# Eight-piece loading of the second half's projection weights over the value steps, and feed-forward weights issued ahead of the values, in a decoder layer

## The reference

```
x = layernorm(x + relative_position_attention(x))     # 16 heads of 32, over the axis of length 8
x = layernorm(x + cross_attention(context, x, mask))  # 8 heads of 64, 512 keys per batch
x = layernorm(x + feed_forward(x))                    # 512 -> 2048 -> 512, relu, fp8-like rounding
```

## Time and profile before

| | |
|---|---|
| median of 3 runs | 1884.73 us (1884.24 to 1888.88) |
| the profiled execution | 1884.78 us |
| its span, first to last instruction | 1883.0 us |
| mean granted TensorE clock | 0.986 of full |
| TensorE busy | 1786.8 us, 95% |
| VectorE busy | 1369.8 us, 73% |
| ScalarE busy | 771.7 us, 41% |
| GpSimd busy | 562.3 us, 30% |
| phase A ends, phase B begins | at about 819 us of the span |

### The profile page before, as it was taken

The page is one execution under the profiler, slowest core; times in us unless marked ns, Lnnn a source line. Parts: engine busy times, 40 slices in busy tenths (PEclk is TensorE's granted clock), DMA queues, the critical chain, the costliest instruction groups (busy, mean ns, idle before and its releaser), DMA issues. The chain is left out here.

```text
span 1883.0 us, 33021 instructions
## 1 busy us (share of the span) xinstructions
PE 1786.8 (95%) x12476; PEld 984.3 (52%) x12476; DVE 1369.8 (73%) x1454; ACT 771.7 (41%) x1208; POOL 562.3 (30%) x576
## 2 busy tenths in 40 slices
PE   6999999999999998977899999999999999999988
PEld 3665455545654564544545545455454554545543
DVE  2899999999899999857556577575775666757621
ACT  3333222322222222237547266373562754736522
POOL 3135865696449525600100302002011020030010
PEclk9999999999999999999999999999999999999999
DMA  9535456525653467666420613606207153061010
GB/s 214 129 76 137 96 135 151 124 76 143 146 118 84 118 167 156 148 148 194 104 71 2 136 51 52 135 1 121 66 9 139 40 85 102 1 130 34 12 34 23
DMA packets 322653, 183.97 MB, mean 98 GB/s; under 512 B 225583, under 2 KB 278831, under 8 KB 322510
## 3 DMA queue, kind: packets, MB, share of 16 engines
q1 hardware_dynamic: 316448, 178.37, 40.7%
q10 hardware_dynamic: 6062, 3.49, 0.9%
HBM read 94.75 MB, written 33.55 MB: 68 GB/s over the span
## 5 line engine op out<-in xcount | busy, mean ns | idle before, releaser
L1178 POOL TENSOR_TENSOR q<-q,x_hi 128x512 f16<-128x512 f32 x28 | 40.5, 1476 | 599.2 <-ACT x_hi L1525 599.2
L1206 PE MATMUL b_ff<-x2T_hi,w1T_hi 128*128 128x512 f16 x512 | 194.6, 380 | 2.3 <-DVE x2T_lo L1616 2.3
L1206 PE MATMUL b_ff<-x2T_hi,w1T_lo 128*128 128x512 f16 x512 | 194.5, 380 | 0.0
L1206 PE MATMUL b_ff<-x2T_lo,w1T_hi 128*128 128x512 f16 x512 | 194.5, 380 | 0.0
L1616 DVE TENSOR_TENSOR p_lo<-k,p_hi 128x1024 f16<-128x1024 f32 x128 | 161.4, 1261 | 37.1 <-ACT p_hi L1471 37.1
L1504 ACT ACTIVATE k<-b_st,mbias 128x512 f32<-128x512 f32 x256 | 161.9, 693 | 40.8 <-PE b_st L1273 37.9
L1666 DVE SCALAR_TENSOR_TENSOR top<-b_st,mleast,top 128x512 f16<-128x512 f32 x168 | 126.1, 751 | 51.4 <-PE b_st L1233 34.4
L785 DVE TENSOR_TENSOR prod<-q,k 128x4096 f32<-128x4096 f32 x32 | 142.2, 4443 | 21.9 <-ACT q L661 21.1
L578 PE MATMUL sm_b<-cT_hi,wsT_hi 128*128 128x256 f16 x512 | 141.7, 277 | 15.1 <-DMA cT_lo<-rows_lo 13.7
L544 PE MATMUL pj_b<-winT_hi,xT_hi 128*128 128x512 f16 x384 | 147.4, 384 | 1.2 <-DVE winT_lo L852 1.2
L544 PE MATMUL pj_b<-winT_lo,xT_hi 128*128 128x512 f16 x384 | 147.2, 383 | 0.0
(11 more groups left out here) (279 smaller groups left out, 4348.2 us busy)
## 6 DMA issues: line engine op xcount, KB each, us to landing
cn<-in_ctx_dram SPq DMA_DIRECT2D x64, 256.0 KB, 3.1
k<-kT_scratch SPq DMA_DIRECT2D x24, 512.0 KB, 7.9
x<-in_x_dram SPq DMA_DIRECT2D x32, 256.0 KB, 3.1
x_scratch<-x SPq DMA_DIRECT2D x32, 256.0 KB, 2.1
q<-x_scratch SPq DMA_DIRECT2D x8, 1024.0 KB, 5.6
q<-x_scratch SPq DMA_DIRECT2D x32, 256.0 KB, 3.0
out_dram<-q SPq DMA_DIRECT2D x32, 256.0 KB, 3.9
xn<-in_x_dram SPq DMA_DIRECT2D x24, 256.0 KB, 2.9
```

What stands on the lines that cost most here:

```text
L1206: mm = pe.matmul(out, a, c, start=(start and n == 0), stop=end)
```

## The change

The load of `tgt_w` (1 MB, one DMA) and of `xout_w` (2 MB, one DMA) at the end of step 56 become eight pieces, one at the end of each of the steps 56 to 63: first four pieces of `tgt_w` of 128 rows (256 KB each), then four of `xout_w` of 128 rows (512 KB each). The piece of step 61 stands ahead of the x1 load of that step. The wait for `sc_done` stays ahead of the first piece. TensorE's waits for the two loads ask for 64 in place of 16. In phase B the issues of the feed-forward weight pairs 0 and 1 (four DMAs of 256 KB) move from behind `load_heads(0, True)` into it, between the keys and the values.

```diff
-                if g == 16 * (NB - 1) + 8 and w.b_ld is not None:
-                    sp.wait_ge(s["sc_done"], 8 * NB)
-                    sp.dma_start(w.wt_n, d.tgt_w.rearrange("(o p) k -> p o k", p=P)).then_inc(w.b_ld["wt"], 16)
-                    sp.dma_start(w.wx_n, d.xout_w.rearrange("(o p) k -> p o k", p=P)).then_inc(w.b_ld["wx"], 16)
+                o = g - 16 * (NB - 1) - 8
+                if 0 <= o < 8 and w.b_ld is not None:
+                    if o == 0:
+                        sp.wait_ge(s["sc_done"], 8 * NB)
+                    rows_of = slice(o % 4 * P, (o % 4 + 1) * P)
+                    if o < 4:
+                        sp.dma_start(w.wt_n[:, o, :], d.tgt_w[rows_of, :]).then_inc(w.b_ld["wt"], 16)
+                    else:
+                        sp.dma_start(w.wx_n[:, o - 4, :], d.xout_w[rows_of, :]).then_inc(w.b_ld["wx"], 16)
...
                 sp.dma_start(k2[0:D2, :, :], k_in[b, 0]).then_inc(s["k_ld"], 16)
                 if first:
+                    for n in range(2):
+                        load_weights(n)
                     sp.wait_ge(s["made"], 1)
...
             load_heads(0, True)
-            for n in range(2):
-                load_weights(n)
...
                 if n in (0, 4):
-                    pe.wait_ge(w.b_ld["wx" if n else "wt"], 16)
+                    pe.wait_ge(w.b_ld["wx" if n else "wt"], 64)
```

## The result

The changed kernel takes 1892.19 us, the median of eight runs (1887.65 to 1896.06); the kernel before, run beside it on the same chip, 1884.52 us (1880.8 to 1888.88). The ratio is 1.0032, 95% interval 1.0018 to 1.0046. The loss is real and small, some 6 us. It is three times what was forecast, and the time lies above the range.

What follows compares the result with a forecast made beforehand. TensorE, busy for 95% of the span, was taken to bound the kernel, so only its idle gaps count. 0.6 (step 57) + 1.4 (step 61), all else 0, gave +2.0 us: 1884.78 to 1886.8, range 1881.3 to 1890.4.

Steps and rivals of the forecast that it cites:

- the 6.39 us hold: SP held by a transpose issued at 699.35 behind the 2 MB wx_n load; hidden, so its removal is worth 0.
- rival A: The gap before 721.26 came from the big loads after all: 1881.8 us, or 1875.9 with the first gap; chance 0.20.
- steps 58 to 60, 62 and 63: Pieces at these steps delay nothing TensorE waits for (3 us of cover for row 59): cost 0.
- the moved weights are worth 0: Second half, weights 0 and 1 ahead of the values: 2.7 us of queue, covered; 0, bounds -1 and +1 us.
- I take 0.6: Step 57, 256 KB piece ahead of row 55's transposes: 0.6 us, between 0.4 (issue alone) and 1.1 (issue and queue).
- I take 1.4: Step 61, 512 KB piece just ahead of the x1 load: 1.4 us of queue, bounds 0.45 and 3.9.
- the rate row: DMA rate of 385 GB/s in the window 700:705, used to size step 61's 0.52 MB at 1.36 us.
- I add 0: Step 61, more slow clock behind the longer gap: 0 in the sum, 1.3 us kept for the range.
- Rival B: A piece blocks transposes behind it for its whole landing, 3.1 us at step 57, 3.9 at 61: 1891.8; chance 0.10.
- Rival C: Nothing on the path: step 57's piece fits queue holes, step 61's x1 load flows as before: 1884.8 us; chance 0.10.
- the early rows_hi: Sign of being right: ScalarE's rows_hi of row 55 comes some 4 us earlier.
- the unmoved restart: Sign of being right: TensorE's restart at 711.15, behind VectorE's stage_lo, stays where it was.

Runs made afterwards that it cites:

- the second one of the same kernel: The changed kernel, unaltered, timed and profiled once more beside a fresh set of the kernel before: 1889.71 us, ratio 1.0035 (1.0023 to 1.0047).

## Why the prediction was wrong

**Right by its steps.** That the big loads of 697 and the 6.39 us hold were hidden, by VectorE's product and GpSimd's long operation: TensorE's restart moved by 0.14 us, and rival A is dead. That steps 58 to 60, 62 and 63 cost next to nothing: the kernel without the piece of 61 stands at 1.0007, of which step 57 is 1.0 us. That the moved weights are worth 0: 0.9995. That the damage is done at step 61, by a piece ahead of the x1 load that row 63's transposes stand behind, and at step 57: shown by putting in the one piece alone, and by taking the x1 load away, with which the changed kernel stands at 0.9998 and the kernel before at 0.9984.

**Wrong by its sizes.** Three terms were too small, and all of one sign.

- "I take 0.6" at step 57: 1.0, near the upper bound of 1.1. The issue and the queue both counted, 0.5 us each, against the reason that the DMA share of 0.62 left holes.
- "I take 1.4" at step 61: the five profiles with a 512 KB piece have a mean of 11.05 us from the residual to quarter 60, against 8.66 in the five with nothing ahead. That is 2.4, inside the bounds 0.45 and 3.9. Two steps failed here. "SP's own 0.45 us run while the queue is full" left the issue out, but the x1 load was issued 0.47 us later in each of the five and quarter 60 keeps its distance to that load's landing; the four small DMAs delay it by their issuing alone. And the rate row gave 1.36 us for the queue where the landing took 1.9 longer. That row is from 700:705; the earlier trace rows has 268 GB/s in 780:785, and by that rate 0.52 MB would be 2.0 us. It is no better as a rule: 1 MB would be 3.9 where 2.2 were found, and 8 KB brought 1.0 and 1.6.
- "I add 0" for more slow clock: from quarter 60 to the second half it takes 37.24 us at the mean of those five, against 35.96 in the five with nothing ahead. (It takes 35.04 or 35.05 in each of the six profiles that show the full clock from 780 to 800.) That is 1.3, the very figure that was kept for the range and left out of the sum. That the dip was there already was no reason for it to stay as long as it was: before, the granted clock is 0.74, 0.92 and 1.00 in the three windows of 5 us from 780 on; with the 512 KB piece alone 0.72, 0.60 and 1.00; after the change 0.71, 0.50 and 0.77.

These are the terms that were mis-sized. They make 1.0 + 2.4 + 1.3 = 4.7 us where 2.0 was forecast, against 6.0 by the first ratio and 6.6 by the second. The rest, 1.3 to 1.9 us, is inside both intervals, and its cause stays open; the start of the second half was at a lower clock after the change (0.74 against 0.84 in 820:840), but the stretch from its first transposes to the first maximum_row matmul lies between 31.3 and 34.2 us in all these kernels without order, so no cause is named for it. The upper end of the range, 1890.4, had both upper bounds but hardly any clock and nothing for this. With the three middles as found, the sum would have been 1889.5: inside the range, and still under the 0.3% from which on the prediction speaks of slower. So the chance of 0.12 for that was too small, since the sum belonged close to the limit, but the right sizes alone would not have put the forecast beyond it.

**The rivals.** Rival B gave 1891.8, nearest to the measured time, and not for its reason. It wanted 3.1 us at step 57, where the seven profiles have 1.0. At step 61 it wanted 3.9; one profile has that (+3.90), the four others with a 512 KB piece lie 1.5 to 2.3 over the mean of 8.66. The Trainium skill, "SBUF — State Buffer", section "The DMA setup-cost knee", gives each transfer about 2 us whatever its size. For a small transfer by itself the trace agrees: the 8 KB pieces landed 2.5 and 2.6 us after their issue, the four of 8 KB in 2.0 at the median. As a price that is paid anew by each transfer in the queue, which was the rival's reading and is not the page's, it is too high at step 57 and wrong for the four small ones, behind which the x1 load landed in 5.7 us. Rival C fell too.

**The wrong signs that weren't.** The prediction named as a refutation any gap that grows by more than 3 us. The gap ahead of quarter 60 did, by 3.89 us, in the first profile, and by 1.36 in the second one of the same kernel. One profile would have spoken for rival B. Of the signs for being right, the early rows_hi (by 3.9 us), the unmoved restart and the waits of the second half came; the gap before quarter 52 was to be 3.5 to 4 us and was 2.49, for the reason given above.

## What to carry to other kernels

A load that is late nowhere gains nothing by being cut up and spread, and each piece is a new chance to stand ahead of something that is late somewhere: look for the transfers that the idle engine waits for, and put nothing ahead of them; here even 8 KB put TensorE's restart off by 1.5 and 2.1 us, of which 0.47 was the issue. Where a gap has a large load just ahead of its transfer, move that load behind the transfer; here this took some 3 us off the kernel before and 6.4 off the changed one, though the change kept a cost of its own. When a gap is going to grow, price the slow clock behind it by the difference between an execution with the dip and one without, and don't take its presence as a reason for zero.

## What the runs showed of the hardware that was not expected

- TensorE's restart behind row 63 follows the landing of the 1 MB load that stands ahead of the transposes, by 1.8 to 2.0 us in fourteen profiles, whatever stands ahead of that load.
- A DMA of 8 KB ahead of the 1 MB load delayed that restart by 1.5 and 2.1 us, one of 512 KB by 1.5 to 2.3 us in four profiles of five and 4.0 in the fifth. Four of 8 KB delayed it by 1.5 us, all of it SP's issuing; the 1 MB load itself landed as fast as with nothing ahead. Why a single 8 KB piece lengthened that landing by 1.0 and 1.6 us and four did not stays open.
- How long SP is held by the issue of a transpose behind those loads is no measure of how late it lands. Behind a 512 KB piece and the 1 MB load the hold by the low transpose of row 63 was 1.62, 1.80, 2.23, 3.02 and 4.47 us; behind 1 MB and 1 MB it was 1.30, where quarter 60 was later than with 512 KB in four profiles of the five.
- A gap of the same length may or may not bring the lower clock. Of four profiles with a gap of 2.74 to 2.90 us ahead of quarter 60, three show it (0.74 in the window of before, 780:785) and take 36.35 to 36.71 us from there to the second half; the fourth, the piece of step 57 alone, has the longest of the four gaps, the full clock and 35.04 us. Its windows of 5 us:

```profile
780.00:785.00 5.00, 2.10 (x15) 1.27 (x14) 4.83 (x4) 0.63 (x1) 4.76 (x4) 1.00 1.12 298
785.00:790.00 5.00, 5.00 (x45) 4.23 (x44) 4.97 (x4) 0.40 (x1) 4.49 (x2) 1.00 0.40 107
```

The nine profiles with a gap of 4.1 us or more took 36.7 to 37.9 us; those with 1.9 us or less, 35.04 or 35.05. So a wait of some 2.8 us costs what the profile prints, and in three cases of four another 1.3 to 1.7.
